# The beta of 36 layer norms moves from the rows to the copy of the turned rows, and every engine's list is ordered anew

## The reference

```python
def _layernorm(x, g, b):                       # first block, norms 1 and 2
    m = jnp.mean(x, axis=-1, keepdims=True)
    v = jnp.mean((x - m) ** 2, axis=-1, keepdims=True)
    return (x - m) / jnp.sqrt(v + EPS) * g + b
...
def _layer_norm(x, g, b):                      # last block, norms 6, 7 and 8
    mean = jnp.mean(x, axis=-1, keepdims=True)
    std = jnp.std(x, axis=-1, keepdims=True, ddof=1)
    return g * (x - mean) / (std + EPS) + b
```

## Time and profile before

| | us |
|---|---|
| median of 3 runs | 972.04 (971.81 to 972.45) |
| the profiled execution | 969.08 |
| its span, first to last instruction | 967.1 |

### The profile page before, as it was taken

How to read it: one execution, slowest core, us unless ns; L and a number is a source line. 1 busy time by engine, 2 the same in 40 slices (tenths; PEclk the granted TensorE clock), 3 DMA queues, 4 the chain that set the end, 5 groups by cost and what they waited for, 6 DMA issues and landing times.

```text
span 967.1 us, 41172 instructions
## 1 busy us (share of the span) xinstructions
PE 891.9 (92%) x18598; PEld 650.9 (67%) x18598; DVE 791.3 (82%) x2202; ACT 603.8 (62%) x890; POOL 321.0 (33%) x389
## 2 busy tenths in 40 slices
PE   8799897899999999999999998889999999999996
PEld 4567665667677678666767766666767777766764
DVE  5899999987567756889898999999666786489896
ACT  6267665677777664455666676757777776445552
POOL 4023244531111113457543324534110112166552
PEclk9899999999999999999999999999999999999999
DMA  8000000000000000000000000000000000000001
GB/s 283 2 25 25 3 3 1 3 3 2 2 4 3 3 14 13 14 13 2 15 24 14 4 3 3 3 3 2 3 2 3 4 3 2 1 2 4 3 13 34
DMA packets 13729, 13.63 MB, mean 14 GB/s; under 512 B 618, under 2 KB 13171, under 8 KB 13299
## 3 DMA queue, kind: packets, MB, share of 16 engines
q1 hardware_dynamic: 13554, 11.00, 3.5%
HBM read 8.91 MB, written 2.10 MB: 11 GB/s over the span
## 4 chain that ended last, share of the span: by engine, by line
PE 43%; DVE 43%; ACT 6%; POOL 3%; issue 2%; DMA 1%; SPq 1%; POOLq 0%; DVEq 0%; ACTq 0%
DVE mx L1421 11%; PE pair L731 9%; PE pair L804 5%; PE pair L969 4%; DVE stats L1144 4%; PE pair L718 4%; PE pair L988 3%; DVE Y L1167 3%; PE pair L964 3%; PE pair L837 3%; DVE Y L1154 2%; DVE X L1299 2%; ACT PT L1065 2%; PE pair L946 2%; PE pair L1002 2%
## 5 line engine op out<-in xcount | busy, mean ns | idle before, releaser
L1065 ACT ACTIVATE PT<-pair 128x1024 f32<-128x1024 f32 x184 | 182.1, 1026 | 99.1 <-PE pair L969 71.1
L1421 DVE TENSOR_REDUCE mx<-pair 128x16 f32<-128x1024 f32 x184 | 217.6, 1215 | 31.0 <-PE pair L969 22.9
L731 PE MATMUL pair<-xf,W_all 128*128 128x512 f32 x336 | 173.4, 620 | 2.5 <-ACT xf L1031 1.6
L1449 POOL TENSOR_SCALAR ve<-mv 128x4 f32<-128x4 f32 x64 | 16.7, 261 | 444.2 <-DVE mv L1147 432.3
L969 PE MATMUL pair<-KQ 32*128 32x128 f32 (+1 forms) x3840 | 117.8, 252 | 6.0 <-ACT PT L1065 3.2
L969 PEld LDWEIGHTS pair<-KQ 32*128 32x128 f32 (+1 forms) x3840 | 106.8, 156 | 24.1 <-ACT PT L1065 4.5
L1031 ACT ACTIVATE KQ<-pair,c 128x512 f32<-128x512 f32 x160 | 100.7, 692 | 22.2 <-PE pair L731 21.7
L1031 ACT ACTIVATE KQ<-pair,cols 128x512 f32<-128x512 f32 x120 | 81.7, 693 | 41.5 <-PE pair L731 40.9
L1031 ACT ACTIVATE V<-pair 64x512 f32<-64x512 f32 x128 | 79.5, 621 | 42.9 <-PE pair L837 41.1
L988 PE MATMUL pair<-PT,V 128*32 128x64 f32 x5120 | 92.9, 222 | 3.7 <-DVE mx L1421 2.4
L988 PEld LDWEIGHTS pair<-PT,V 128*32 128x32 f32 x5120 | 77.0, 110 | 22.2 <-issue 5.5
(11 more groups left out here) (126 smaller groups left out, 1690.1 us busy)
## 6 DMA issues: line engine op xcount, KB each, us to landing
W_all<-weights SPq DMA_DIRECT2D x1, 2880.0 KB, 12.9
Xin<-x SPq DMA_DIRECT2D x8, 256.0 KB, 3.0
C<-ctx SPq DMA_DIRECT2D x8, 256.0 KB, 4.0
out<-X SPq DMA_DIRECT2D x8, 256.0 KB, 2.3
row<-rows SPq DMA_DIRECT2D x1, 1024.0 KB, 6.1
c<-const SPq DMA_DIRECT2D x1, 390.0 KB, 5.7
W_all<-weights SPq DMA_DIRECT2D x1, 192.0 KB, 3.0
c<-const SPq DMA_DIRECT2D x1, 93.0 KB, 2.0
```

The costliest lines, as they stand in the source:

```text
L731: pe.matmul(t[:, 0:TOK], W(name), src[:], start=True, stop=True).then_inc(*banks.full(*use))
L1065: act.activation(PT[:, place, :], banks.of("B", a, s, v)[:], ACT.Exp, scale=float((D // (2 * PAIRS[a])) ** -0.5)).then_inc(*banks.drain((" ...
L1421: dve.tensor_reduce(dst, banks.of("A", a, s, v)[:].rearrange("p (u m t) -> p u m t", u=2, t=S), AX.X, ALU.max).then_inc(*banks.drain(("A", ...
```

## The change

PE's `x1` no longer waits for the beta. POOL's step `n1` now only scales (`Y = Y * rstd`), PE turns `Y`, and ACT's copy adds beta as a bias for each partition. POOL adds beta to the rows in a step of its own, `beta`, later in its list: `X = Y + beta`. A new step `0.1.0 betas` turns the five beta rows once: PE waits for the DMA of `row` and does five transposes, and ACT picks one column of each into a small tile `beta`. ACT's `ff` and DVE's `z`, which overwrite `Y`, now wait for POOL's `beta`. All five lists are ordered anew; PE's list holds 54 fillings in 24 steps where there were 73 in 30. The fillings, the `betas` step and POOL's 36 `beta` steps are the only steps that are not in both lists. What follows is the diff without most of the lists.

```diff
     "PE": """
-        0.0.0 x@0; 0.0.1 x@1+8; 0.0.0 pq@0 pk@1; 0.0.3 x@2+5; 0.0.1 pq@3; 0.0.2 x@0; 0.0.0 first@1; 0.0.3 pv@2; 0.0.0
-        length@3; 0.0.2 pq@0; 0.0.0 maskrow@1; 0.0.2 pk@3; 0.0.3 pk@2; 0.0.0 A0@02; 0.0.2 pv@3; 0.0.0 pv@6; 0.0.3
+        0.0.0 x@0; 0.1.0 betas@1; 0.0.0 pk@0 pq@2; 0.0.1 x@3 pq@0+3; 0.0.0 first@2+1 length@0+1; 0.0.2 x@2; 0.0.0
+        maskrow@0; 0.0.3 x@3; 0.0.0 A0@23+2; 0.0.2 pq@0; 0.0.0 A1@13; 0.0.1 pk@1; 0.0.3 pk@0; 0.0.1 pv@2; 0.0.2 pk@3;
...
     "ACT": """
-        0.0.0 x; 0.0.1 x; 0.0.0 qpair0 qpair1 Kpar; 0.0.3 x; 0.0.1 qpair0; 0.0.2 x; 0.0.1 qpair1; 0.0.3 pv; 0.0.2
+        0.0.0 x Kpar; 0.0.1 x; 0.0.0 qpair0 qpair1; 0.0.1 qpair0 qpair1; 0.0.3 x; 0.0.2 x qpair0; 0.1.0 betas; 0.0.2
...
     "DVE": """
-        0.0.0 qm; 0.0.1 qm; 0.0.2 qm; 0.0.3 qm; 0.0.0 qf nz; 0.0.1 qf; 0.0.0 lm lrow; 0.0.2 qf; 0.0.0 mx1 mx0; 0.1.0
-        split; 0.0.0 mx3; 0.0.3 qf; 0.0.2 nz; 0.0.1 nz; 0.0.0 mx2 nm; 0.0.3 nz; 0.0.2 lm; 0.0.1 lm; 0.0.0 mrow; 0.0.2
...
     "POOL": """
+        0.1.0 sum n1 beta; 0.2.0 kvstats; 0.1.1 sum n1 beta; 0.2.1 kvstats; 0.1.3 sum n1 beta; 0.1.2 sum n1 beta;
...
+        down; 0.6.0 n1 beta leaky; 0.5.3 addwo down; 0.6.1 sum n1 beta; 0.6.2 sum n1; 0.6.1 leaky; 0.6.2 beta leaky;
...
+BETAS = ["n1_b", "n2_b", "e6_b", "e7_b", "e8_b"]
...
+        beta = sb("beta", [P, len(BETAS)])
...
                     elif name == "x1":
-                        once.wait_ge(*(vec if a == 8 and section.group == GROUPS - 1 else pool).at("x1", a, s))
-                        turn(X[s], use)
+                        if a == 8 and section.group == GROUPS - 1:
+                            once.wait_ge(*vec.at("x1", a, s))
+                            turn(X[s], use)
+                        else:
+                            once.wait_ge(*pool.at("scaled", "x1", a, s))
+                            turn(Y[s], use)
+                    elif name == "betas":
+                        once.wait_ge(*row_in.at())
+                        t = room(*use)
+                        for k, beta_row in enumerate(BETAS):
+                            mm = pe.transpose(t[:, 96 * k:96 * k + 128], rowb(beta_row), K32("ident"))
+                        mm.then_inc(*banks.full(*use))
...
+                    elif name == "betas":
+                        move(beta[:], full.rearrange("p (k c) -> p k c", c=96)[:, :, 0], use, *use)
+                    elif name == "x1" and not (a == 8 and section.group == GROUPS - 1):
+                        k = BETAS.index(f"n{a}_b" if a < 3 else f"e{a}_b")
+                        once.wait_ge(*operand.at("betas", 1, 0, ago=section.group))
+                        move(xf[s][:], full, use, *use, f=ACT.Identity, bias=beta[:, k:k + 1])
...
                     elif name == "ff":
+                        if not (a == 8 and section.group == GROUPS - 1):
+                            once.wait_ge(*pool.at("x1", a, s))
...
                     elif name == "z":
+                        once.wait_ge(*pool.at("x1", a, s))
...
-                def affine(name, *tag):
+                def scale(*tag):
...
+                    g_.tensor_tensor(Y[s][:], Y[s][:], rstd[lane(tag)][:].unsqueeze(2).broadcast_to((P, NT, 128)),
+                                     ALU.mult).then_inc(*pool.mark("scaled", *tag))
+
+                def add_beta(name, *tag):
...
-                    g_.tensor_tensor(X[s][:], X[s][:], rowb(name + "_b").unsqueeze(1).broadcast_to((P, NT, 128)),
+                    g_.tensor_tensor(X[s][:], Y[s][:], rowb(name + "_b").unsqueeze(1).broadcast_to((P, NT, 128)),
                                      ALU.add).then_inc(*pool.mark(*tag))
```

More of the change, by code:

```diff
@@ L58 @@
[L58 to L67, removed]
@@ new lines @@
+        maskrow@2; 0.5.1 pv@0; 0.1.1 B0@23 B1@10; 0.1.2 length@4; 0.1.1 v0@5; 0.1.2 maskrow@4; 0.5.0 maskrow@6; 0.1.1
+        v1; 0.1.2 A0@01; 0.1.1 v2@7 v3; 0.2.0 x1@6; 0.1.2 A1@02; 0.1.1 t0@6; 0.3.3 ctx@2; 0.3.2 ctx@3; 0.1.1 t1@7;
+        0.2.0 fc1@4; 0.2.1 pv@5; 0.5.1 maskrow@4; 0.2.3 kv@6; 0.1.2 maxrow@3; 0.2.1 pk@0; 0.1.2 B0@13; 0.2.0 fc2@4;
+        0.1.2 B1@01 v0@5 v1; 0.1.3 A0@30; 0.1.2 v2@4 v3; 0.1.3 A1@10; 0.5.2 pv@5; 0.1.2 t0@6; 0.2.1 x1@7; 0.5.3 pv@0;
+        0.2.1 fc1@1; 0.2.2 pv@5; 0.1.3 maxrow@0; 0.1.2 t1@4; 0.2.0 q@1; 0.2.1 fc2@2; 0.2.0 pq@3+1; 0.1.3 B0@03; 0.2.2
@@ new lines @@
+        1.2.1 pv@1; 1.1.2 maxrow@4; 1.3.3 ctx@5; 1.2.0 fc1@6; 1.5.3 pv@3; 1.2.1 pk@0; 1.5.1 ksum@1; 1.1.3 length@2;
+        1.2.0 fc2@4; 1.1.2 B0@13; 1.1.3 maskrow@1; 1.2.1 x1@5+2; 1.2.0 pv@6; 1.1.2 v0@7 v1; 1.1.3 A0@01; 1.5.2 pv@4;
+        1.1.3 A1@03; 1.2.1 fc1@5; 1.5.0 pv@2; 1.2.1 fc2@3; 1.1.2 B1@02; 1.2.3 kv@6; 1.5.0 maskrow@7; 1.5.3 ksum@4;
+        1.5.1 pv@5; 1.1.3 maxrow@3; 1.1.2 v2@4 v3; 1.2.2 pv@2; 1.5.1 maskrow@5; 1.1.2 t0@4; 1.2.0 q@7; 1.5.2 ksum@3;
+        1.2.2 pk@0; 1.1.2 t1@1; 1.1.3 B0@12; 1.5.2 maskrow@0; 1.2.0 pq@6; 1.1.3 B1@10 v0@7 v1; 1.2.1 q@6; 1.2.0 A0@12;
@@ L323 @@
-        leaky; 1.7.1 sum; 1.7.0 leaky; 1.7.1 n1; 1.7.2 sum n1; 1.7.1 leaky; 1.7.2 leaky; 1.7.3 sum n1; 1.8.0 sum;
-        1.7.3 leaky; 1.8.1 sum; 1.8.2 sum; 1.8.3 sum
+        0.1.0 sum n1 beta; 0.2.0 kvstats; 0.1.1 sum n1 beta; 0.2.1 kvstats; 0.1.3 sum n1 beta; 0.1.2 sum n1 beta;
+        0.2.2 kvstats; 0.2.3 kvstats; 0.2.0 sum n1 beta; 0.2.1 sum n1 beta; 0.2.0 z n3 n3q; 0.2.2 sum n1 beta; 0.2.1 z
+        n3 n3q; 0.2.2 z n3 n3q; 0.3.1 wo; 0.3.0 wo; 0.2.3 sum n1 beta z; 0.3.0 down; 0.2.3 n3 n3q; 0.3.2 wo; 0.3.0
@@ new lines @@
+        addff; 0.3.1 down addff; 0.3.2 down; 0.3.3 wo; 0.3.2 addff; 0.3.3 down; 0.4.0 addwo; 0.3.3 addff; 0.4.1 addwo;
+        0.4.2 addwo; 0.5.0 addwo; 0.4.3 addwo; 0.5.0 down; 0.5.1 addwo; 0.5.2 addwo; 0.5.1 down; 0.6.0 sum; 0.5.2
+        down; 0.6.0 n1 beta leaky; 0.5.3 addwo down; 0.6.1 sum n1 beta; 0.6.2 sum n1; 0.6.1 leaky; 0.6.2 beta leaky;
+        0.7.0 sum n1 beta leaky; 0.6.3 sum n1 beta; 0.7.1 sum n1; 0.6.3 leaky; 0.7.1 beta; 0.7.2 sum n1; 0.7.1 leaky;
+        0.7.2 beta leaky; 0.8.0 sum n1 beta; 0.7.3 sum n1 beta; 0.8.0 leaky; 0.7.3 leaky; 0.8.1 sum n1 beta; 0.8.2 sum
@@ new lines @@
+        n1 beta; 0.8.3 sum; 0.8.1 leaky; 0.8.3 n1; 0.8.2 leaky; 0.8.3 beta leaky; 1.1.0 sum n1 beta; 1.2.0 kvstats;
+        1.1.1 sum n1 beta; 1.1.2 sum n1 beta; 1.2.1 kvstats; 1.1.3 sum n1 beta; 1.2.2 kvstats; 1.2.3 kvstats; 1.2.0
+        sum n1 beta; 1.2.1 sum n1 beta; 1.2.0 z n3 n3q; 1.2.1 z n3 n3q; 1.2.2 sum n1 beta; 1.3.0 wo; 1.2.3 sum; 1.3.1
+        wo; 1.2.3 n1 beta; 1.2.2 z n3 n3q; 1.2.3 z n3 n3q; 1.3.0 down; 1.3.1 down; 1.3.2 wo; 1.3.3 wo; 1.3.0 addff;
+        1.3.1 addff; 1.3.2 down; 1.3.3 down; 1.3.2 addff; 1.3.3 addff; 1.4.0 addwo; 1.4.1 addwo; 1.4.2 addwo; 1.4.3
@@ L325 @@
+        addwo; 1.5.0 addwo; 1.5.1 addwo; 1.5.2 addwo; 1.5.0 down; 1.5.1 down; 1.5.2 down; 1.5.3 addwo down; 1.6.0 sum
+        n1 beta; 1.6.1 sum n1; 1.6.0 leaky; 1.6.1 beta leaky; 1.6.2 sum n1 beta leaky; 1.6.3 sum n1 beta; 1.7.0 sum
+        n1; 1.6.3 leaky; 1.7.0 beta leaky; 1.7.1 sum n1 beta; 1.7.2 sum n1 beta; 1.7.1 leaky; 1.7.2 leaky; 1.7.3 sum
+        n1; 1.8.0 sum; 1.7.3 beta leaky; 1.8.1 sum; 1.8.2 sum; 1.8.3 sum
     """,
@@ L1054, in step @@
                         once.wait_ge(*pool.at("zero", s))
-                    full = banks.of(*use)[:, 0:TOK] if name in (
+                    full = banks.of(*use)[:, 0:96 * len(BETAS)] if name == "betas" else banks.of(*use)[:, 0:TOK] if name in (
                         "ctx", "x", "x1", "q", "kv", "fc1", "o", "ff", "pk", "pq", "pv", "up0", "up1", "up2", "up3"
```

495 lines of the change are left out of this document (241 added, 254 removed).

## The result

| | before | after |
|---|---|---|
| median, us | 971.92 (970.88 to 972.45) | 958.76 (958.26 to 959.65) |
| the profiled execution, us | 969.08 | 958.26 |
| its span, us | 967.1 | 956.3 |

The ratio is 0.9867 (95% interval 0.985 to 0.9884): the changed kernel is 1.3% faster, where the forecast was 0.4% slower. In the code of after, PE's turns stand in L718, `betas` in L786, ACT's copies in L1041, POOL's scaling in L1487 and its addition of beta in L1496. In the kernels of the experiments the same lines are shifted by a few.

The account below looks back on a forecast made before the run. No single engine was taken as the limit: DVE full from 42 to 200 us, PE from 200 to 400 and 700 to 930, both nearly from 400 to 600. 972.0 + 8 (start) - 4 (move and order) = 976.0 us; range 967 to 984.

Parts of the forecast that it names:

- The start: Up to 42 us: PE's `betas`, second in its list, waits for the DMA of `row`; 8 us slower, between 5.5 and 10.
- three ways to price it: First score late by 8.3 us (PE's old first steps), 6.8 (new list's durations) or 10 (slower PE clock added).
- the walk along the new list: At the start, the new list's steps summed with the old rows' durations: first score at about 25.1 us, 6.8 late.
- One sign: On PE after the wait for `row`: granted clock near 0.5 for some us.
- the lower clock that was forecast: PE's first steps after the 10.8 us wait run at the 1.2 GHz level, taking 3 us longer in all.
- The body: After the start: moving beta off PE's path and the new order together gain 4 us, from PE's direct waits.
- the open time at 40.6 us: Idle time of the fuller engine, PE or DVE, by stretch from 42 to 930 us; a better order takes only from this.
- faster by the order alone: Rival: new lists overlap streams better at 400 to 500 and 600 to 700 us; gain 13.5 us, time 966.5; chance 0.26.
- Its other remark: Where PE is called full, its weight loads are busy only 143.2 of 200 and 163.2 of 230 us, so room may remain.
- three signs of being wrong: PE passes `betas` without waiting; a lag at 42 us is gone at 200; 400 to 700 us shortens by over 8.
- a wait for ACT's `ff`: Rival: in seven norms ACT's `ff` waits for one more POOL addition, 1.3 us each, 9 in all: 985 us; chance 0.09.
- The move does nothing: Rival: taking POOL's addition off PE's path gains 0, time 980 us; counted within the forecast, no chance of its own.

Follow-up runs that it names:

- late `betas`: The changed kernel with the `betas` step moved in PE's list from second place to behind the first stream's A0; 951.16 us, ratio 0.9792.
- the sooner `row`: The changed kernel with SP issuing the load of `row` ahead of the four context tiles, `betas` still second; 955.72 us, ratio 0.985.

## Why the prediction was wrong

**The start was right.** PE's wait, its end (15.68 us; forecast 16.2), the first maximum 7.3 us late (forecast 7 to 10) and the lag still there at 200 us came as predicted. The term was 8 us, between 5.5 and 10. Taken out again, it was 0.9867 - 0.9792 = 0.75% or 7.3 us, and 6.8 us between the two profiled spans. Of the three ways to price it, the walk along the new list (6.8 us) was best. That it is so close is in part luck: it took the first matmuls at full speed, and they were 1.7 us slower (see below).

One sign can't be read as the prediction meant it. The granted clock was to stand near 0.5 behind the wait; the table by stretch shows 1.00 from 16.8 to 19.9 us:

```profile
16.80:19.90 3.10, 3.10 (x7) 1.00 0.94 401
```

But the trace of after has no record of the clock ahead of 19.20 us, and the table counts time without a record as 1.00. The first record, of 1.00, begins at 7.88 us in the kernel before, at 9.13 with late `betas`, at 16.27 with the sooner `row`. In all four kernels the matmuls that start ahead of it are slow and those behind it are not. So here the durations are the evidence: in after 3.07 us for what takes 1.98 in the earlier trace rows, and 1.33 us for the five transposes that take 0.77 in the kernel with late `betas`. They speak for the lower clock that was forecast, at a price of 1.1 + 0.6 = 1.7 us instead of 3; but the kernel with late `betas` pays most of it as well (3.46 us). The Trainium skill ("TensorE: Matmul & The Clock Gate", Part 1) has the throttled clock as the default; the slow first matmuls of all these kernels agree, with or without the wait.

**The body was mis-sized, and that decided the sign.** The prediction took 4 us for the move and the order together. Measured without the start, it was 0.0208 x 972 = 20 us: 13 for the order alone, 7 for the move under it. Two steps of the working failed.

- *The order was priced at nothing of its own.* The prediction put it into the 4 us that were the waits for the addition. It also put the open time at 40.6 us, as the idle time of the fuller engine in each stretch. That left out the time outside 42 to 930 us and counted the fillings as work; PE's open time was 99.3 us. "A better order can take only from this" was the right rule with too small a sum. Still, the 20 us would have fitted even into the 40.6: what failed is the step that took 4 of them, and with no reason but the waits. Where DVE was the fuller engine the bound may hold: the columns show no gain in layers 0 to 2 of either group. Where PE was, in layers 3 to 8, the gain came.
- *The move was priced from the waits of the old trace.* These waits say what the addition costs under the old lists. Read rightly they are 2.3 us in 6 and not 4.0 in 7, since the seventh gap was no wait for it, and there the answer, 1.8 us, was about right. The new lists rely on the earlier rows: with the old beta under them PE waits 24.4 us in 20 turns, and the time is 7 us longer. The worth of a shorter path was a product of the two edits and can't be read from a trace that has neither.

**The rival that came true** was *faster by the order alone*, at 966.5 us with a chance of 0.26 and a gain of 13.5 us against a start of 8. The order alone gave 13 us and the start cost 7, and the move added its 7 us on top. That 13.5 and 13 agree is luck: 13.5 was a third of the 40.6 us, a share that no row gave. Nor did the order need the shorter path that the rival put it down to; it gained its 13 us with the addition back in the path. Of the two stretches that it named, the first was right: of the 16.9 us that the column of after gains from 203 us to the end of the span, 5.8 fall between 391 and 472 us. From 472 to 668 us nothing is gained, some 9 us come from stretches where PE was called full, and 2 from the tail. Its other remark was nearer to those: that PE's weight loads, at 143.2 of 200 us and 163.2 of 230 us, left more room than PE's busy time showed. They now reach 146.5 and 165.4 us in the same stretches. The Trainium skill ("Perfetto Trace Analysis", Identifying the Most-Contended Engine) takes the weight loads' share as the better measure of room; these rows agree with it.

**The signs.** None of the three signs of being wrong came up. PE did wait, the lag was still there at 200 us, and between 391 and 668 us the column of after gains 5.9 us, where more than 8 between 400 and 700 was the sign. They watched the start and one stretch, and the gain was spread.

**The other rivals.** POOL didn't become a wait for ACT's `ff`: the trace of after has no wait of ACT for POOL's addition. "The move does nothing" was nearly true of the old lists and false of the new.

**The smaller steps.** ACT's copy with beta was priced at 693 ns and lasts 687 (groups by line and shape of after); the copy of `betas`, bounded by 0 and 0.6 us, lasts 0.17 us:

```profile
L1041 ACT ACTIVATE xf<-pair 128x512 f32<-128x512 f32 x44 | 26.1, 597 | 28.0 <-PE pair L718 27.7
...
L1041 ACT ACTIVATE xf<-pair,beta 128x512 f32<-128x512 f32 x36 | 24.6, 687 | 14.0 <-PE pair L718 13.7
...
L1041 ACT ACTIVATE beta<-pair 128x5 f32<-128x5 f32 x1 | 0.2, 167 | 0.0
```

DVE's 2.5 us of waits for the finished rows, which were to stay, are gone as well: PE's weight loads alone wait for the addition in after. That is within the size of the other terms.

**What stays open.** The order's 13 us (9.8 by the spans) are located by layer, but not by list: which of the five lists brings them, or which steps, was not tried. The one attempt to gain by moving a kind of step by hand lost 26 us.

## What to carry to other kernels

When engines walk fixed lists, a trace prices an edit only under its own order: a shorter path was worth 1.8 us under the old lists and 7 us under lists written for it, so price "edit plus new order" as a case of its own, with the engine's open time (idle time and fillings) as an outer bound. An early wait ahead of everything in an engine's list was a debt paid in full here: 6.9 us at layer 0 was 6.8 us at the end under the new lists, and 10.8 was 9.7 under the old. So look first at what the second instruction of a list waits for, and move it behind work that needs nothing.

## What was unexpected of the hardware

- The first four large matmuls of an execution lasted 3.07, 3.22 and 3.46 us in three kernels, after waits of 10.30, 6.99 and 0.84 us, where the earlier trace rows has 1.98 us behind eight fillings. The length of the wait ahead of them made no difference that shows.
- The table's column of the granted clock read 1.00 over those 3.07 us, because the trace has no record of the clock ahead of 19.20 us. Ahead of the first record go by durations.
- Taking out all the fillings moved the time by -0.07% and +0.2%, though the mean granted clock fell from 0.991 to 0.977 and from 0.988 to 0.980.
- The same 1 MB load of `row`, issued 5.2 us sooner and ahead of the context tiles, took 8.2 us to land instead of 6.1.
